# Choosing, ranking, weighing and placing the first two groups of chunks in one round of wider instructions

## The reference

```python
q = elu(x @ Wq.T) + 1;  k = elu(x @ Wk.T) + 1;  v = x @ Wv.T          # per head
kv_cumsum = cumsum(k[..., :, None] * v[..., None, :], axis=tokens)
out = q @ kv_cumsum / max(q . cumsum(k), 1e-6)
x = layernorm(x + out @ Wo.T)
logits = (rms_normalised(x) * router_scale) @ router_w                # 8 logits per token
top_k_idx = top_k(logits, 2)
combine = the two experts' softmax weights, renormalised, * per_expert_scale
out = sum over the two experts of combine * (gelu(x @ gate0_e) * (x @ gate1_e)) @ linear_e
x = layernorm(x + out)
```

## Time and profile before

| | us |
|---|---|
| median of 3 runs | 218.0 (217.31 to 218.88) |
| the profiled execution, its time | 217.45 |
| its span in the profile | 215.6 |
| TensorE busy (PE) | 162.0, 780 matmuls |
| VectorE busy (DVE) | 145.8, 517 instructions |
| GpSimd busy (POOL) | 133.3, 119 instructions |
| ScalarE busy (ACT) | 92.0, 310 instructions |
| the 32 scatters (L471) on GpSimd | 31.2 |

### The profile page before, as it was taken

One profiled execution on the slowest core, in us unless ns is written; L12 is line 12 of the kernel. 1 busy time (PEld: TensorE's weight loads), 2 busy tenths in 40 slices (PEclk: granted clock), 3 DMA queues, 4 the chain that ended last, 5 costly groups with the idle time before them and its releaser, 6 DMA issues.

```text
span 215.6 us, 3402 instructions
## 1 busy us (share of the span) xinstructions
PE 162.0 (75%) x780; PEld 117.3 (54%) x780; DVE 145.8 (68%) x517; ACT 92.0 (43%) x310; POOL 133.3 (62%) x119
## 2 busy tenths in 40 slices
PE   3698997776998689866549980998599999970540
PEld 0355654445575366545328660886488888850430
DVE  0469999999989967998634880277256666622580
ACT  2324674454236432433365440255255666610280
POOL 6585469199545998376087557777246666661570
PEclk9999999998599958997556996599889999999597
DMA  5849400000000001001411102653443311115741
GB/s 156 227 95 378 183 27 15 12 5 8 0 2 28 25 13 38 26 24 55 89 47 49 37 29 79 161 155 102 112 110 101 90 53 46 49 37 168 240 136 53
DMA packets 18626, 17.56 MB, mean 81 GB/s; under 512 B 2880, under 2 KB 16192, under 8 KB 18480
## 3 DMA queue, kind: packets, MB, share of 16 engines
q1 hardware_dynamic: 16304, 12.66, 20.6%
q0 software_dynamic: 2304, 4.69, 6.8%
HBM read 10.62 MB, written 6.73 MB: 80 GB/s over the span
## 4 chain that ended last, share of the span: by engine, by line
PE 47%; DVE 21%; ACT 9%; issue 9%; DMA 6%; SPq 3%; POOL 2%; DVEq 0%; POOLq 0%; ACTq 0%
PE bank L727 9%; DVE prod L980 5%; PE bank L562 5%; PE bank L713 4%; PE bank L549 4%; PE bank L715 4%; PE bank L714 4%; DVE num L987 4%; PE bank L735 4%; ACT rows L814 3%; ACT junk L806 2%; DMA pl<-both 2%; PE bank L704 2%; SPq L387 2%; PE bank L603 2%
## 5 line engine op out<-in xcount | busy, mean ns | idle before, releaser
L513 POOL DMA_INDIRECT both<-yout,zin x39 | 37.6, 965 | 21.9 <-DVE yout L1254 18.6
L471 POOL DMA_INDIRECT zbuf<-rows,slot x32 | 31.2, 976 | 21.0 <-DVE slot L1124 13.0
L457 POOL TENSOR_TENSOR kv<-v,qk 128x1152 f32<-128x1152 f32 x16 | 35.0, 2190 | 12.3 <-DVE qk L954 12.3
L562 PE MATMUL bank<-kv,C 128*128 128x432 f32 (+1 forms) x96 | 37.2, 528 | 0.0
L727 PEld LDWEIGHTS bank<-w_l,actT 128*128 128x128 f32 x156 | 22.5, 203 | 8.9 <-issue 8.1
L727 PE MATMUL bank<-w_l,actT 128*128 x156 | 26.2, 294 | 1.4 <-ACT actT L905 1.1
L562 PEld LDWEIGHTS bank<-kv,C 128*128 128x128 f32 x96 | 18.9, 211 | 15.2 <-issue 14.5
L980 DVE TENSOR_TENSOR prod<-bank,qk 128x432 f32<-128x432 f32 (+1 forms) x48 | 24.1, 546 | 0.8 <-PE bank L562 0.6
L1254 DVE COPY yout<-bank 128x128 f32<-128x128 f32 x39 | 11.3, 291 | 19.6 <-PE bank L727 19.6
L713 PE MATMUL bank<-w_hi,zin_hi 128*128 x39 | 20.3, 520 | 3.1 <-DVE zin_lo L1239 3.0
L987 DVE TENSOR_REDUCE num<-prod 128x144 f32<-128x1152 f32 x16 | 21.6, 1353 | 0.5
(11 more groups left out here) (137 smaller groups left out, 318.1 us busy)
## 6 DMA issues: line engine op xcount, KB each, us to landing
zin<-zbuf SPq DMA_DIRECT2D x39, 65.0 KB, 1.9
w_g<-in_gate_w SPq DMA_DIRECT2D x4, 512.0 KB, 6.1
pl<-both SPq DMA_DIRECT2D x8, 256.0 KB, 5.3
xTs<-in_xT SPq DMA_DIRECT2D x16, 64.0 KB, 2.3
w_l<-in_lin_w SPq DMA_DIRECT2D x1, 1024.0 KB, 9.4
out<-pl SPq DMA_DIRECT2D x8, 128.0 KB, 1.8
both<-yout,zin POOLq DMA_INDIRECT x39, 2.3
zbuf<-pads SPq DMA_DIRECT2D x8, 65.0 KB
```

The lines of the kernel that those rows point to most:

```text
L457: pool.tensor_tensor(kv[:, s, :].rearrange("p (h e d) -> p h e d", e=HE, d=HD), a, b, ALU.mult).then_inc(kv_done, 1)
L471: pool.indirect_dma_start(zbuf, bass.IndirectOffsetOnAxis(ap=slot[:, g, r, j:j + 1].bitcast(U32), axis=0), rows[:, GROUP * g + j, r, :], N ...
L513: pool.indirect_dma_start(both, bass.IndirectOffsetOnAxis(ap=zin[:, b, D + 1:D + 2].bitcast(U32), axis=0), yout[:, b, :], None).then_inc(p ...
L562: pe.matmul(pre_ps[b][:, 0:c1 - c0], const("tri"), kv[:, s, c0:c1], start=True, stop=True)\
```

## The change

Groups 0 and 1 are chosen, ranked, weighed and placed together, as 8 chunks, when group 1's turn comes (`routed(1)` is chunks 0 to 7, `count(1)` is 8). Statistics, normalised rows and logits stay by four: group 0's logits are copied into the first half of `lgs`, group 1's into the second. In the steps of route 2 and 3 of g = 1, `choose`, `exp_logits`, `ranks` and `weigh_and_place` are left out; in those of g = 2 they work on 64 instead of 32 numbers per partition (128 instead of 64 for both experts), and `ranks` has ten matmuls instead of six. The tiles that hold these values are twice as wide. GpSimd writes the 16 scatters of both groups in g = 3: two before `roots(2)`, fourteen after it.

```diff
+        def routed(g):
+            return slice(0 if g == 1 else GROUP * g, GROUP * g + GROUP)
+        def count(g):
+            return routed(g).stop - routed(g).start
...
-                for g in (range(0, 2), range(2, 3), range(3, 4))[p]:
-                    sp.wait_ge(scattered[g], 16 * K * GROUP)
+                for g in (range(1, 2), range(2, 3), range(3, 4))[p]:
+                    sp.wait_ge(scattered[g], 16 * K * count(g))
...
-                    if g >= 2:
-                        scatter(g - 2, (0,))
+                    if g == 3:
+                        scatter(1, (0,))
                     roots(g - 1)
...
-                if route == 0 and g >= 2:
-                    scatter(g - 2, (1,))
-                if route == 2 and g >= 2:
-                    scatter(g - 2, (2, 3))
+                if route == 1 and g == 3:
+                    scatter(1, range(1, 2 * GROUP))
...
-                pe.wait_ge(ind_done, g + 1)
-                if g:
-                    pe.wait_ge(rank_used, g)
+                pe.wait_ge(ind_done, g)
+                if g > 1:
+                    pe.wait_ge(rank_used, g - 1)
...
-                for by in range(1, GROUP + 1):
+                for by in range(1, chunks + 1):
...
-                if route == 3:
+                if route == 3 and g > 1:
                     ranks(g - 1)
                 elif exists(g, m - 1):
                     inter(g, m - 1)
...
+                c = slice(GROUP, 2 * GROUP) if g == 1 else slice(0, GROUP)
+                ac.copy(lgs[:, c, :].rearrange("p c e -> p (c e)"), last_lg_ps if is_last(g) else lg_ps)\
...
-                    exp_logits(g - 1)
+                    if g > 1:
+                        exp_logits(g - 1)
...
-                    if route is not None:
+                    if route is not None and (route < 2 or g > 1):
                         parts[route](g - 1, i)
```

More of the change, by code:

```diff
@@ L53 @@
 _at = 0
-for _name, _n in (("tri", P), ("stri", P), ("ident", P), ("ones", P), ("block", H * HE), ("desc", GROUP * E),
+for _name, _n in (("tri", P), ("stri", P), ("ident", P), ("ones", P), ("block", H * HE), ("desc", 2 * GROUP * E),
                   ("tok", CHUNKS * K), ("ebase", E), ("tile", MOST), ("row", MOST), ("euler", GROUP), ("half", 2 * GROUP), ("pad", PADS)):
@@ L342, in rank_of @@
         def rank_of(g):
-            return last_rank_ps if g == GROUPS - 1 else rank_ps
+            return (last_rank_ps if is_last(g) else rank_ps)[:, 0:(count(g) + 1) * E]
         def tiles(eng, *stages, beside=lambda k: None):
@@ L464, in roots, with scatter @@
                                    const("half").rearrange("p (k c) -> p k c", k=2), ALU.pow).then_inc(root_done, 1)
-            def scatter(g, part=range(GROUP)):
-                pool.wait_ge(route_done, g + 1)
+            def scatter(g, part):
+                pool.wait_ge(route_done, g)
                 for j in part:
+                    c = routed(g).start + j
                     for r in range(K):
                         pool.indirect_dma_start(
-                            zbuf, bass.IndirectOffsetOnAxis(ap=slot[:, g, r, j:j + 1].bitcast(U32), axis=0),
-                            rows[:, GROUP * g + j, r, :], None).then_inc(scattered[g], 16)
+                            zbuf, bass.IndirectOffsetOnAxis(ap=slot[:, r, c:c + 1].bitcast(U32), axis=0),
+                            rows[:, c, r, :], None).then_inc(scattered[g], 16)
             def split_low(parts):
@@ L518, in _ @@
                 place(k)
-            pool.wait_ge(dlog_done, GROUPS)
-            pool.tensor_tensor(R1["elog"][:, :], const("euler"), R1["dlog"][:, :], ALU.pow).then_inc(elog_done, 1)
+            pool.wait_ge(dlog_done, last)
+            pool.tensor_tensor(R1["elog"][:, 0:GROUP], const("euler"), R1["dlog"][:, 0:GROUP], ALU.pow).then_inc(elog_done, 1)
             for k in range(POW_AT, ROWS_AT):
                 place(k)
-            scatter(last)
+            scatter(last, range(GROUP))
             for k in range(ROWS_AT, TILES):
@@ L682, in step @@
                     put_out(g, m - 2)
-                if route == 3 and exists(g, m - 1):
-                    pe.wait_ge(rank_used, g)
+                if route == 3 and g > 1 and exists(g, m - 1):
+                    pe.wait_ge(rank_used, g - 1)
                     inter(g, m - 1)
@@ L722, in output @@
                 if k == QUOTA[-2]:
-                    pe.wait_ge(rank_used, GROUPS)
+                    pe.wait_ge(rank_used, last)
                 after(pe, yout_done, k if k <= QUOTA[-2] else k - 1)
@@ L749, in _ @@
             pe.wait_ge(act_in, 3 * CHUNKS)
-            pe.wait_ge(rank_used, last)
+            pe.wait_ge(rank_used, last - 1)
             look_up(0)
@@ L1071, in choose @@
             def choose(g, i):
[L1072 removed]
+                n, A = count(g), of(g)
+                logit = lgs[:, 0:n, :]
+                desc = const("desc")[:, 0:n * E].rearrange("p (c e) -> p c e", e=E)
                 if i == 3:
@@ L1094, in choose @@
                     st.ready(1)
-                    ve.tensor_tensor(ind[:, :].rearrange("p (c e) -> p c e", e=E), A["ind1"], A["ind2"],
+                    ve.tensor_tensor(ind[:, 0:n * E].rearrange("p (c e) -> p c e", e=E), A["ind1"], A["ind2"],
                                      ALU.add).then_inc(ind_done, 1)
                     st.ready()
-                    ve.tensor_tensor(A["dlog"], A["gap"], root[:, g, 1], ALU.mult).then_inc(dlog_done, 1)
+                    rms = root[:, routed(g).start // GROUP:g + 1, 1]
@@ L1117, in weigh_and_place @@
-                    reduce(pe_of[:, :, :], pe12[:, :, :, :], ALU.add, last=1)
+                    inverse(w_n[:, 0], A["esum"], last=1)
+                    reduce(pe_of_n, pe_n, ALU.add, last=1)
                 if i == 5:
-                    tt(w12[:, 1], w12[:, 0], A["elog"], ALU.mult, last=1)
+                    tt(w_n[:, 1], w_n[:, 0], A["elog"], ALU.mult, last=1)
                 if i == 6:
-                    tt(rows[:, cols(g), :, D].rearrange("p c r -> p r c"), w12[:, :, :], pe_of[:, :, :], ALU.mult)
+                    tt(rows[:, routed(g), :, D].rearrange("p c r -> p r c"), w_n, pe_of_n, ALU.mult)
@@ L1227, in beside @@
                 if k == 7:
-                    ve.wait_ge(rank_used, GROUPS)
+                    ve.wait_ge(rank_used, last)
                     ve.tensor_copy(cnt_i[:, :], base2[:, :]).then_inc(cnt_done, 1)
```

69 lines of the change are left out of this document (36 added, 33 removed).

## The result

The changed kernel took 220.21 us (median of 20 runs, 217.98 to 222.77) against 217.63 us before (20 runs, 215.92 to 219.31): ratio 1.0111, 95% interval 1.0082 to 1.0139, so 2.4 us (1.8 to 3.0) slower. The ratio is that of the runs within 1.5% of the fastest of their kernel, so it differs a little from that of the medians, which lie 2.6 us apart. The forecast was 221.8 us, slower. The profiled execution took 218.5 us (span 216.7), at the low end of its kernel, so its rows are read in pieces: from `roots(0)` (43.34; before 42.92), to `roots(2)`, to the first load, to `turn_last_z`, to the end. The lines answering L954, L980, L987 on VectorE are now L964, L990, L997.

The account below looks back on a forecast made before the run. Bounds: TensorE's half-clock sums at chunk 8 and the expert tiles' start behind the scatters. Profiled 217.45 + 4.0 (`turn_last_z`) - 0.2 (clock) = 221.25, or 221.8 us against the runs' 218.0; range 219.7 to 223.6.

Parts of the forecast that it names:

- the burst: GpSimd behind `roots(2)`: 14 scatters without a gap instead of 6, making `turn_last_z` 4.0 us later.
- the wide round: Routing of groups 0 and 1 together: 1.3 us gained, 0.5 lost, so `roots(2)` 0.8 us earlier.
- 1.3 us earlier: VectorE from chunk 9 on: 0.77 us without the wait for ranks, 0.55 from `num` to the next `qk`.
- the clock rises earlier: Chunk 8's sums on TensorE: gain 2.5 us instead of 1.3 if the clock rises halfway through them.
- Features of chunk 14, at nothing: VectorE's feature instruction, held up to about 1 us by GpSimd's products, costed at nothing because 1.72 us idle follows.
- 0.5 us later: Group 1's routing: wider `weigh_and_place` instructions 0.3 us, more and wider rank matmuls 0.2; between 0.3 and 1.0.
- 10.2 us later: First load of `zin` on SyncE: eight more scatters behind `roots(2)` at 1.28 us each.
- What of it is hidden: Start of the expert tiles: with the later load, `turn_last_z` runs at 117.4 against 113.42, only 4.0 us later.
- 0.2 off: TensorE in the tiles, without its 0.50 us gap, gets full clock sooner: 0.2 us less, between -0.6 and +0.5.
- the first (all of VectorE's saving arrives): At `roots(2)` 5.1 us arrive instead of 0.8, so no change: 217.7 us; chance 0.14.
- The second (the clock holds by itself): TensorE stays at full clock at 52 us and before the tiles, so faster: 215.6 us; chance 0.06.
- The last rival: Only the weighing is gained, width costs 1.0: -0.5 us at `roots(2)`, 223.1 us, or 223.8 with clock's +0.5; chance 0.06.

Follow-up runs that it names:

- the scatters alone: Kernel before with only group 0's scatters moved to where the changed kernel has them, two ahead of `roots(2)`, six behind it: 222.45 us, ratio 1.0303.
- the second profile: The changed kernel run again as it is, compared with the kernel before: 220.13 us, ratio 1.0154.
- Held at full clock: Changed kernel with unused TensorE matmuls in all waits around group 0's logits: 217.63 us, 1.0052; the kernel before with the same: 218.29 us, 1.0046.

## Why the prediction was right

It said slower by the burst, and that is shown: the scatters alone cost 3.0%, the rest of the change takes part of it back. How close the number came owes something to luck: the wide round gives 2.3 us by the medians and 2.6 to 3.1 by the profiles, where the forecast had 0.8, and by the medians the burst's price was put 1.0 too low, which takes part of that error back. In the second profile the marks of the forecast are nearly met (`roots(2)` 91.66 for 91.4, first load 112.49 for 112.4, `turn_last_z` 117.31 for 117.4), but its `roots(0)` starts 1.2 us later than before; in the first they come 1.3 to 1.5 us too early, and the `qk` behind chunk 8 already comes 1.1 too early (61.16 for 62.3). Term by term, by the profiles of the two kernels (the changed one twice):

- **"1.3 us earlier" at chunk 8**: right for the clock of the profile it was drawn from. At a mean clock of 0.57 `num` comes 0.80 us earlier (16.77 for 17.57), and 0.54 follow from `num` to `qk`: 1.34. But the reading behind it, that the sums on TensorE set chunk 8 whatever VectorE did, was barely true of the kernel before at half clock and not at all at full clock: `prod` began behind VectorE's choosing, at 15.2 us after `roots(0)` whatever the clock, and the half-clock sums held the three by 0.1 us (1.58 for 1.48). Choosing and half-clock sums were nearly level, so that freeing VectorE gains as much as TensorE's clock allows, and the clock was taken as given. It runs otherwise from execution to execution, and the changed kernel feels that more than the one before did. In the two profiles of the changed kernel the gain was 2.8 and 1.9 us against the profile of before, and its own sign of being wrong, sums that end well before 59 us, came in the first (58.07). This is the step that was mis-sized; the prediction named the case (the clock rises earlier) and put it at the edge of its range. Its 2.5 us for it should be 2.2, since half of 3.61 us at twice the speed saves 0.9.
- **Why the clock falls**: the prediction took TensorE's idle time from 47.30 to 49.30 as the reason. With that time filled the clock still fell; it held only when the short waits around the logits were filled too.
- **Features of chunk 14, at nothing**: held by 0.81 us, covered, as said.
- **"0.5 us later" by width**: from the `qk` behind chunk 8 to `roots(2)` 28.64 us before (28.76 to 28.91 in its variants), 28.91 and 28.85 after (29.07 to 29.17 in its variants with two scatters ahead): 0 to 0.5.
- **"10.2 us later"**: from `roots(2)` to the first load 10.80 before, 20.80 and 20.83 after: 10.0.
- **What of it is hidden**: from the load to `turn_last_z` 10.42 before, 5.17 and 4.82 after, so 5.3 to 5.6 hidden; forecast 5.4 (9.4 later at the load, 4.0 at `turn_last_z`). In its sum 112.4 and 2.15 make 114.55, not 114.7, which is too little to matter.
- **Clock, "0.2 off"**: from `turn_last_z` to the end of the span 102.2 us before, 100.7 in both profiles after. Of these 1.5 us 0.6 lie in phase 0 (21.64 us at 0.82, 21.00 at 0.91); the other 0.9 behind it are not traced to a place.

From `roots(0)` to the end of the span that makes 172.7 us before and 173.4 and 173.9 after, 0.7 and 1.2 us more, where the forecast's terms make 3.8. The medians of 20 runs differ by 2.6, over many courses of the clock; the clock was low in the profile of before at both places (0.57 at chunk 8, 0.82 in phase 0), which makes the difference of the profiles smaller. The error of the forecast, 1.2 us too slow, has the sign of the two mis-sized terms, chunk 8 and the end; how the runs share it between them, and what the price of the burst takes back, was not measured.

Of the rivals, the first (all of VectorE's saving arrives) needs TensorE out of the way. Held at full clock, the gain up to `num` is 2.7 us, 3.2 with the 0.54 behind it, not 5.6: `prod` still waits 1.18 us. The second (the clock holds by itself) did not come: both profiles after have the half clock at chunk 8 and at the start of the tiles. The last rival's +0.5 was beaten in every profile but the one at 0.50. The Trainium skill, "Perfetto Trace Analysis", section "Optimizing Scalar/DVE Operations", says that grouping can pay where the engine is saturated; by its 60 ns for each of the 23 instructions that is an estimated 1.4 us here. The runs show 3.2 us at full clock and 1.34 at 0.57: what grouping is worth here hangs on TensorE, not on the number of instructions.

## What to carry to other kernels

Work taken off one engine is worth what the next one allows: before crediting it, look whether the engine waited for would be late by itself, and at which clock. Grouping work also groups what hangs on its result: eight indirect DMAs that used to run beside the attention became 10 us in front of a load. And where a clock varies, compare stretches at the same granted clock, not single profiles.

## What was not expected of the hardware

- The same program runs at several mean clocks. In its 20 runs the changed kernel took 217.98 to 218.97 us in the seven at 0.882 or 0.883, 219.79 to 220.45 in the seven at 0.875 or 0.876, and 220.40 to 222.77 in the six below. Where the half clock falls decides up to 3.6 us at chunk 8 (14.26 to 17.84, in profiles of the changed kernel and its variants) and 2.4 us in phase 0. Why it falls at other places in other executions is open.
- TensorE's clock fell to half although its long wait was filled: in the changed kernel with ten unused matmuls the engine worked from 47 to 51 us without a gap, then stood idle only in waits of 0.28 to 0.35 us (0.72, 0.73 and 0.64 us busy in three us), and was at half clock from 54. With unused matmuls in those waits too it stayed at 1.00 up to 59 us.
- Sixteen 128x128 fp32 matmuls (32 records) took 4.82 us on a clock that rose under them. That cost nothing where TensorE waited 6.9 us, and 22 outlasted the wait.
